# First windowed attention and two expert mixtures: K masked in blocks of 32 rows, row sums from a column of ones, the w3 half scaled on ScalarE, bias, mask and sum on GpSimd

## The reference

```python
# windowed attention: 16 heads of 8, windows of 64, each looks at itself and the window before
q, k, v = x @ Wq.T + bq, x @ Wk.T + bk, x @ Wv.T + bv
scores = einsum('bchqd,bckhd->bchqk', qc, kc) / sqrt(8)      # 64 queries against 128 keys
attn = softmax(where(valid, scores, -1e9))                   # valid: the first window of a sequence has none before it
out = einsum('bchqk,bckhd->bcqhd', attn, vc) @ Wo.T + bo
# mixture: 8 experts, the two best are used, weight s_e of the token for expert e
h  = silu((x * s_e) @ w1[e].T + b1[e])
x2 = h @ w2[e].T + b2[e]
x3 = (x * s_e) @ w3[e].T + b3[e]
y  = sum over e of x2 * x3 * mask_e
z  = (silu(x @ sw1.T) * (x @ sw2.T)) @ sw3.T                 # shared expert
out = y + z
```

## Time and profile before

| | us |
|---|---|
| median of three executions | 4510.75 |
| lowest, highest | 4509.15, 4514.94 |
| the profiled execution, whole | 4523.47 |
| its span in the profile | 4522.2 |
| windowed attention, 28.2 to 280.4 | 252.2 |
| first mixture with its norm, after its loads | 202.5 |
| second mixture with its loads | 216.0 |

### The profile page before, as it was taken

One profiled execution on the slowest core, in us unless ns is written; L12 is line 12 of the kernel. 1 busy time (PEld: TensorE's weight loads), 2 busy tenths in 40 slices (PEclk: granted clock), 3 DMA queues, 4 the chain that ended last, 5 costly groups with the idle time before them and its releaser, 6 DMA issues. The chain is left out here.

```text
span 4522.2 us, 158903 instructions
## 1 busy us (share of the span) xinstructions
PE 3865.6 (85%) x66864; PEld 2684.5 (59%) x66864; DVE 3250.0 (72%) x6705; ACT 2515.7 (56%) x4761; POOL 2493.9 (55%) x2057
## 2 busy tenths in 40 slices
PE   6858767279999999999999732899999999999996
PEld 3435544146766666666666521666666666766764
DVE  6749659577777777777778436777777777777773
ACT  2323323046767667667676401666676666767664
POOL 2211111077767677677767302766766767767662
PEclk8769979689999999999999855999999999999998
DMA  0010010033233333333322201333323333233222
GB/s 14 1 32 1 3 32 2 4 87 91 65 92 82 78 88 80 80 78 89 81 70 68 59 8 34 80 79 80 90 65 93 79 81 91 65 92 82 63 70 53
DMA packets 307779, 280.49 MB, mean 62 GB/s; under 512 B 158840, under 2 KB 205696, under 8 KB 307072
## 3 DMA queue, kind: packets, MB, share of 16 engines
q1 hardware_dynamic: 307072, 270.33, 23.5%
HBM read 55.22 MB, written 1.05 MB: 12 GB/s over the span
## 5 line engine op out<-in xcount | busy, mean ns | idle before, releaser
L1375 ACT ACTIVATE l_sq<-PS 128x512 f32<-128x512 f32 x384 | 225.9, 595 | 200.6 <-PE PS L1228 160.9
L1375 ACT ACTIVATE m_sq<-PS 128x512 f32<-128x512 f32 x384 | 225.9, 595 | 196.1 <-PE PS L1228 158.3
L1640 POOL TENSOR_TENSOR l_Pm<-l_Pm,l_rs 128x1024 f32<-128x1024 f32 x96 | 182.7, 1903 | 238.9 <-DVE l_rs L1512 238.9
L1640 POOL TENSOR_TENSOR m_Pm<-m_Pm,m_rs 128x1024 f32<-128x1024 f32 x96 | 182.7, 1904 | 236.7 <-DVE m_rs L1512 236.7
L124 POOL TENSOR_TENSOR rstd<-rstd,minus_half 128x4 f32<-128x4 f32 x40 | 41.7, 1044 | 398.1 <-DVE rstd L120 398.1
L1530 DVE TENSOR_TENSOR XN<-PS,XN 128x128 f32<-128x128 f32 x192 | 56.1, 292 | 273.0 <-PE PS L1280 273.0
L1499 DVE TENSOR_TENSOR l_QR<-PS,l_rot 128x512 f32<-128x512 f32 x192 | 131.7, 686 | 165.5 <-ACT l_sq L1375 165.5
L1499 DVE TENSOR_TENSOR m_QR<-PS,m_rot 128x512 f32<-128x512 f32 x192 | 131.8, 686 | 164.3 <-ACT m_sq L1375 164.3
L1635 POOL TENSOR_TENSOR l_QR<-l_QR,l_UQ 128x1024 f32<-128x1024 f32 x96 | 227.8, 2372 | 25.0 <-DVE l_UQ L1502 25.0
L1635 POOL TENSOR_TENSOR m_QR<-m_QR,m_UQ 128x1024 f32<-128x1024 f32 x96 | 227.7, 2372 | 24.6 <-DVE m_UQ L1502 24.6
L1635 POOL TENSOR_TENSOR l_KR<-l_KR,l_UK 128x1024 f32<-128x1024 f32 x96 | 226.8, 2362 | 0.6 <-DVE l_UK L1502 0.6
(11 more groups left out here) (387 smaller groups left out, 11817.4 us busy)
## 6 DMA issues: line engine op xcount, KB each, us to landing
l_V<-l_Vt SPq DMA_DIRECT2D x576, 128.0 KB
m_V<-m_Vt SPq DMA_DIRECT2D x576, 128.0 KB
l_V<-l_Vt SPq DMA_DIRECT2D x384, 64.0 KB
m_V<-m_Vt SPq DMA_DIRECT2D x384, 64.0 KB
l_wqkv<-l_wqkv_dram SPq DMA_DIRECT2D x72, 128.0 KB, 2.4
m_wqkv<-l_wqkv_dram SPq DMA_DIRECT2D x72, 128.0 KB, 2.4
l_rot<-l_rot_dram SPq DMA_DIRECT2D x24, 256.0 KB, 3.6
m_rot<-l_rot_dram SPq DMA_DIRECT2D x24, 256.0 KB, 3.7
```

The costliest lines, as they stand in the source:

```text
L1375: ac.activation(sq[:, c, b * 512:(b + 1) * 512], PS[:, 2 * c + b, :], ACT.Square).then_inc(sq_out)
L1640: gp.tensor_tensor(pm, pm, over(rs[:, :], 2, [P, 16, 2 * LW]), ALU.mult).then_inc(pn_out)
```

## The change

In the attention the mask has four columns in place of 16 and repeats every 32 rows. kTm then holds four copies, made by GpSimd alone, and head 4g+j is row block g (32 rows) of copy j. `scores` is one call for two banks: four matmuls of 32 rows by 64 columns by 512. v gets a ninth column of ones for each head, set once at the start, so that the value matmul yields the row's sum in its ninth column; `sums` is gone. Softmax works on halves of eight heads. The stages of a tile are spread over more turns of the loop: values run two tiles behind the scores, the transpose of the output three, the output matmul and the addition to X four; v's projection goes to bank 2, values to bank 1, the output's transpose to bank 0 and the output to bank 3. At the start of the program one fence and one wait are gone, and the attention's weights are issued behind x directly.

In the mixture w1 products fill banks 0 and 1 and w3 products banks 2 and 3. VectorE takes out the w1 half only. ScalarE takes out the w3 half, with the scale; GpSimd adds b3, multiplies by the mask, and later adds up the eight experts in three steps and adds the result to X. The shared expert's second matmul moves behind the next tile's transposes. The four gate groups get banks of their own and are taken out after the norm loop, and the choice of experts moves behind VectorE's part of the first tile.

```diff
-                headmask = sl("headmask", P, A_H)
+                headmask = sl("headmask", P, 4)
                 qT = sl("qT", P, 2, P)
                 kT = sl("kT", P, W_K)
-                kTm = sl("kTm", P, 2, A_H, W_K)
-                vc = sl("vc", P, 3, 2, D)
+                kTm = sl("kTm", P, 2, 4, W_K)
+                vc = sl("vc", P, VR, 2, A_H, A_DH + 1)
                 S = sl("S", P, 2, A_H, P)
-                pT = sl("pT", P, A_H, P)
-                mx, sm, rs = sl("mx", P, A_H), sl("sm", P, A_H), sl("rs", P, A_H)
+                pT = sl("pT", P, 2, A_H, P)
+                mx, rs = sl("mx", P, A_H), sl("rs", P, A_H)
...
+                G.step(gp.memset(vc[:, :, :, :, :], 1.0))
+                G.wait()
+                for dst, src in ((wq[:, :], t["a_wqT"]), (wk[:, :], t["a_wkT"]), (wv[:, :], t["a_wvT"]), (wo[:, :], t["a_woT"]),
+                                 (headmask[:, :], t["a_headmask"]), (bq[:, :], column("a_bq")), (bk[:, :], column("a_bk")),
+                                 (bv[:, :], row("a_bv", D)), (bo[:, :], row("a_bo", D))):
+                    sp.dma_start(dst, src).then_inc(loaded, 16)
+                sp.wait_ge(loaded, 16 * 11)
...
+                            for g in (2 * k, 2 * k + 1):
+                                rows = slice(32 * g, 32 * g + 32)
+                                m = te.matmul(PS[A_WIN * c:A_WIN * (c + 1), 4 + g, :], qT[rows, par, A_WIN * c:A_WIN * (c + 1)],
+                                              kTm[rows, par, :, A_WIN * c:A_WIN * c + P], start=True, stop=True)
...
+                        if n == 0:
+                            te.wait_ge(vc_out, min(i + 3, NT))
+                        if i >= 3 and n == 1:
+                            te.wait_ge(add_out, i - 2)
...
+                    for i in range(NT + 4):
+                        turned, valued, out = 1 <= i <= NT, 2 <= i < NT + 2, 3 <= i < NT + 3
...
+                    def exponent(i, k):
+                        sh = S[:, i % 2, 8 * k:8 * k + 8, :]
+                        ac.wait_ge(sub_out, 2 * i + k + 1)
+                        ac.activation(sh, sh, ACT.Exp, scale=float(A_DH) ** -0.5).then_inc(exp_out)
+
+                    def turned(i, n):
+                        ac.wait_ge(p_turn, 4 * i + n + 1)
+                        if i >= 2:
+                            ac.wait_ge(pv_mm, i - 1)
+                        ac.copy(pT[:, i % 2, 4 * n:4 * n + 4, :].rearrange("p a b -> p (a b)"), PS[:, 2 + n % 2, :]).then_inc(pT_out)
...
+                        for c in range(2):
+                            m = ve.tensor_tensor(vc[:, i % VR, c, :, 0:A_DH], PS[:, 2, c * P:(c + 1) * P].rearrange("p (h d) -> p h d", h=A_H),
+                                                 bv[:, :].rearrange("p (h d) -> p h d", h=A_H), ALU.add)
+                        m.then_inc(vc_out)
...
+                        V.step(ve.reciprocal(rs[:, :], got[:, :, A_DH]))
...
+                        if 3 <= i < NT + 3:
+                            divide(i - 3)
+                        if i < NT:
+                            softmax(i, 0)
+                        if i >= 4:
+                            residual(i - 4)
+                        if i < NT:
+                            softmax(i, 1)
+                        if i + 2 < NT:
+                            values_copy(i + 2)
...
-                        gp.tensor_tensor(kTm[:, par, 10:, :], over(kT[:, :], 1, [P, A_H - 10, W_K]),
-                                         over(headmask[:, 10:], 2, [P, A_H - 10, W_K]), ALU.mult).then_inc(km2_out)
-                        if i == 0:
+                            gp.wait_ge(sc_mm, 2 * (i - 1))
+                        gp.tensor_tensor(kTm[:, par, :, :], over(kT[:, :], 1, [P, 4, W_K]),
+                                         over(headmask[:, :], 2, [P, 4, W_K]), ALU.mult).then_inc(km_out)
+                        if i == 1:
...
                             turn(i - 1)
+                            shared_down(i - 1)
                         if i < NT:
                             up(i)
                         if i:
                             down(i - 1)
                         if i < NT:
-                            shared(i)
+                            shared_turn(i)
...
+                            if i >= 2:
+                                ac.wait_ge(y3_out, i - 1)
+                            if i == 0:
+                                ac.wait_ge(mask_out, 1)
+                            for n in range(2):
+                                for e in range(4 * n, 4 * n + 4):
+                                    m = ac.activation(x3[:, i % 2, e, :], PS[:, 2 + n, (e % 4) * D:(e % 4 + 1) * D], ACT.Copy, scale=sc[:, i, e:e + 1])
+                                m.then_inc(x3_out)
                             ac.wait_ge(sg_turn, i + 1)
+                            if i >= 1:
+                                ac.wait_ge(z_mm, i)
...
+                        for n in range(2):
+                            ve.wait_ge(up_mm, 5 * i + n + 1)
+                            for e in range(4 * n, 4 * n + 4):
+                                m = ve.scalar_tensor_tensor(hin[:, i % 2, e, :], PS[:, n, (e % 4) * D:(e % 4 + 1) * D], sc[:, i, e:e + 1], b1[:, e, :],
+                                                            ALU.mult, ALU.add)
+                            m.then_inc(hin_out)
...
-                        ve.tensor_tensor(y8[:, :, :], y8[:, :, :], x3[:, i % 2, :, :], ALU.mult).then_inc(x3_used)
-                        ve.wait_ge(x3_used, i + 1)
-                        V.step(ve.tensor_reduce(y1[:, :], y8[:, :, :].rearrange("p e d -> p d e"), AX, ALU.add))
-                        V.wait()
-                        ve.wait_ge(zadd_out, i + 1)
-                        V.step(ve.tensor_tensor(X[:, i, :], X[:, i, :], y1[:, :], ALU.add))
+                        ve.tensor_tensor(y, y, x3[:, i % 2, :, :], ALU.mult).then_inc(y3_out)
...
+                    for g in range(NG):
                         ve.wait_ge(gate_mm, g + 1)
-                        ve.tensor_copy(sc[:, 4 * g:4 * g + 4, :], PS[:, 1 + g % 2, 0:4 * E_N].rearrange("p (j e) -> p j e", j=4)).then_inc(gate_out)
-                    choose()
+                        ve.tensor_copy(sc[:, 4 * g:4 * g + 4, :], PS[:, 1 + g, 0:4 * E_N].rearrange("p (j e) -> p j e", j=4)).then_inc(gate_out)
+                    ve.wait_ge(gate_out, NG)
+                    scores()
+                    for i in range(NT + 1):
+                        if i:
+                            ve.wait_ge(z_mm, i)
+                            ve.tensor_tensor(X[:, i - 1, :], PS[:, 4, I_SH:I_SH + D], X[:, i - 1, :], ALU.add).then_inc(zadd_out)
+                        if i < NT:
+                            up(i)
+                            gated(i)
+                        if i == 0:
+                            choose()
+                        if i:
+                            down(i - 1)
...
+                            x = x3[:, i % 2, :, :]
+                            gp.wait_ge(x3_out, 2 * i + 2)
+                            G.step(gp.tensor_tensor(x, x, b3[:, :, :], ALU.add))
+                            G.wait()
+                            gp.tensor_tensor(x, x, over(mask[:, i, :], 2, [P, E_N, D]), ALU.mult).then_inc(x3m_out)
                         if i:
-                            down(i - 1)
-                        if i < NT:
-                            ve.wait_ge(z_mm, i + 1)
-                            ve.tensor_tensor(X[:, i, :], PS[:, 4, I_SH:I_SH + D], X[:, i, :], ALU.add).then_inc(zadd_out)
-
-                def pool():
-                    for g in range(NG):
-                        norm_root(g)
-                    for i in range(NT):
-                        gp.wait_ge(x3_out, 4 * i + 4)
-                        gp.tensor_tensor(x3[:, i % 2, :, :], x3[:, i % 2, :, :], over(mask[:, i, :], 2, [P, E_N, D]), ALU.mult).then_inc(x3m_out)
+                            y = y8[:, (i - 1) % 2, :, :]
+                            gp.wait_ge(y3_out, i)
+                            for n in (4, 2, 1):
+                                G.step(gp.tensor_tensor(y[:, 0:n, :], y[:, 0:n, :], y[:, n:2 * n, :], ALU.add))
+                                G.wait()
+                            gp.wait_ge(zadd_out, i)
+                            gp.tensor_tensor(X[:, i - 1, :], X[:, i - 1, :], y[:, 0, :], ALU.add).then_inc(tree_out)
...
-    c["a_headmask"] = (np.arange(P)[:, None] // A_DH == np.arange(A_H)[None, :]).astype(f)
+    c["a_headmask"] = (np.arange(P)[:, None] % 32 // A_DH == np.arange(4)[None, :]).astype(f)
```

More of the change, by code:

```diff
@@ L208, in project, with scores @@
                         te.matmul(PS[:, 0, P:P + W_K], wk[:, :], xw(i, 0, W_K), start=True, stop=True).then_inc(qk_mm)
[L209 to L215 removed]
+                    def scores(i, k):
                         par = i % 2
```

306 lines of the change are left out of this document (151 added, 155 removed).

## The result

| | before | after |
|---|---|---|
| median, us | 4512.84 (4509.15 to 4515.95, 4 executions) | 4435.85 (4432.96 to 4439.44, 4 executions) |
| ratio, 95% interval | | 0.983 (0.982 to 0.985) |
| span of the profiled execution | 4522.2 | 4438.1 |
| attention ends (the mixture's gate weights are loaded) | 280.4 | 253.6 |
| first mixture, loads included | 216.6 | 190.1 |

The account below looks back on a forecast made before the run. It took a ring through all engines to set the attention's tile and VectorE to bound the mixture. Attention and start 96.8 plus mixtures 42.6 make 139.4 off 4523.5, 4384; medians lying 12.7 lower, 4371 us; range 4340 to 4412.

Parts of the forecast that it names:

- So a full turn is 8.6 + 1.2: Attention: 8.6 us of TensorE work plus a 1.2 us stall awaiting the addition to X, rounded to 10.0.
- four filling turns: Attention's first turns, two paced by VectorE's 6 us and by masking the sequence's first window: 22.4 us in all.
- Rival B: Attention: TensorE's clock stays at 0.80, a turn takes 11.9 us, 25 us more, total 4396; chance 0.20.
- Rival F: Attention and mixture: many small pieces keep TensorE at 1.2 GHz; slower, 4620 at share 0.8; chance 0.03.
- Scores in row blocks: Attention: a scores call of eight 512-column matmul instructions, its four pieces side by side, takes 1.1 us.
- rival D: Attention scores: the 32-row pieces run only in pairs, 18 us more, total 4389; chance 0.10.
- GpSimd's mask: Attention: GpSimd makes the whole mask in 2.7 or 1.4 us, beside other work, costed at nothing.
- VectorE's pieces of 1024: Attention softmax: maximum and subtraction in four instructions of 1024 columns, 1.22 us each, 4.9 together.
- The start: Program start: first weight load from 8.59 to about 3.9, first arithmetic from 16.31 to 12.0, 4.3 us less.
- The mixture's tile: Mixture: 8.8 us in place of 10.12, paced by GpSimd's 7.6 plus 1.2 of mutual waiting with VectorE.
- rival C: Mixture: GpSimd and VectorE do not wait for each other, TensorE paces at 8.2 us, total 4354; chance 0.12.
- The mixture's sum: Per mixture: 6.6 + 14 x (10.12 - 8.8) - 3.8 = 21.3 us less; two make 42.6.

Follow-up runs that it names:

- experiment 1: Changed kernel with the output matmul ahead of the first scores and the addition to X ahead of the first softmax half: 4358.99 us, ratio 0.965.
- experiment 6: Changed kernel with three unread 256-column matmuls on TensorE ahead of its wait for the addition to X: 4380.92 us, ratio 0.969.
- experiment 9: Changed kernel with one unread 256-column matmul ahead of the wait for the addition to X: median 4417.98 us, profiled execution 4352.14.
- Experiment 7: Changed kernel, stall kept, with each score matmul contracting all 128 rows instead of 32: 4402.00 us, ratio 0.974.
- experiment 10: experiment 1 with VectorE doing each mixture's last-tile b3, mask, expert sum and addition to X: median 4339.35 us; profiled execution 4441.55.
- experiment 5: Changed attention and program start, with the mixture of the kernel before: 4497.39 us, ratio 0.996.
- experiment 8: Changed kernel with GpSimd's addition of b3 in the mixture left out: 4426.15 us, ratio 0.980.
- experiment 2: Changed kernel, stall kept, with value matmuls moving 32 columns per head in place of 9: 4420.28 us, ratio 0.980.

## Why the prediction was wrong, point by point

- **The failed step** is "So a full turn is 8.6 + 1.2", in the part on the attention, which the sum takes as 10.0 us: the turns took 15.1, at a granted clock of 0.50. Work and stall were nearly right: 8.2 us at full clock (experiment 1) and a stall of 1.21. What failed is that the stall was added as time and not also weighed as what takes the clock away. Experiments 1 and 6 show it: without the stall, or with the stall filled, the clock stays at 1.00 in the stage's middle.
- **What the step would have given.** The execution of experiment 9 that kept its clock and most of its waiting puts the attention's end at 186.7 us. The prediction put it at 280.4 - 96.8 = 183.6, so the sum for a kept clock was right within 3 us, in part by luck. Its full turns take 9.6 us in place of 10.0, but the four filling turns take 31.3 (first maximum of the first and of the fifth tile at 29.49 and 60.77) in place of 22.4, some of it at the low clock.
- **Rival B** (the clock stays at the attention's present 0.80) took a mean over the stage for a property of it. In the earlier trace rows the clock falls to 0.53 and is back at 1.00 within a tile, when the 128-row scores follow. Experiment 7 has 128-row scores behind the same stall and reads 0.93. The change removed what brought the clock back. I had put the fall down to four microseconds of short work alone, but TensorE also stood idle in them: 1.16 us before the values (in the earlier trace rows, one tile on), and then

```profile
102.70 0.33 PE L252 MATMUL PS<-ident,a_o 128*128 128x128 f32 x1 [0.92 <-DVE a_o L356]
103.39 0.80 PE L254 MATMUL PS<-a_wo,a_oT 128*128 128x128 f32 x2 [0.35 <-ACT a_oT L301]
```

  The output's transpose takes 0.33 us, as it does at full clock in the changed kernel, and the output matmul behind it 0.80, as at the low one. So the trace of before already had a clock that fell behind an idle microsecond.
- **Rival F** named the mechanism, small pieces at 1.2 GHz, with chance 0.03, because it was tied to the mixture too and priced at 4620. In the attention alone, 13 turns of 15.1 in place of 10.0 (the prediction's count) cost 66 of the 70 us missed there. Against it I had set the 1.00 "of most of the attention tile", which was 128-row work. The Trainium skill, TensorE: Matmul & The Clock Gate, section "Part 1: The HAM clock gate (the "warmup" mystery)", lets an array that stays busy have its full clock back; here 192 us without a gap did not bring it back (experiment 10; 191.3 of 192 us busy in experiment 5), so busy in the profile's sense is not what the gate goes by.
- **Scores in row blocks:** the forecast of 1.1 was right and rival D fell: 1.09 us a call, the four pieces run side by side, and 1.98 at half the clock.
- **GpSimd's mask:** 1.467 us, near the lower price (1.4); VectorE no longer works on K beside it.
- **VectorE's pieces of 1024:** 1.225 us, as worked out from the earlier trace rows.
- **The start:** the first weight load at 4.00, the first arithmetic at 12.34, 4.0 us earlier; 4.3 forecast.
- **The mixture's tile** was mis-sized: 8.8 forecast, 8.03 measured, against

```profile
L623 DVE TENSOR_TENSOR f_sg<-f_sg,PS x16: 420/422/423, 294.8 to 425.0; 128x256 f32<-128x256 f32 x16
```

  whose second is at 312.04: 112.96 us for 14 tiles, 8.07 each. GpSimd does not set it (experiment 8), TensorE does. The waiting for each other is real, but smaller:

```profile
L635 DVE TENSOR_TENSOR f_y<-f_y,f_x x16: 1226/1576/3386, 314.2 to 435.7; 128x1024 f32<-128x1024 f32 x16
L666 POOL TENSOR_TENSOR f_x<-f_x,f_b x16: 2341/2358/3336, 303.8 to 431.3; 128x1024 f32<-128x1024 f32 x16
```

```profile
L673 POOL TENSOR_TENSOR f_y<-f_y 128x256 f32<-128x256 f32 x14 | 16.3, 1166 | 1.1
L673 POOL TENSOR_TENSOR f_y<-f_y 128x128 f32<-128x128 f32 x13 | 8.6, 660 | 1.0
L676 POOL TENSOR_TENSOR X<-X,f_y 128x128 f32<-128x128 f32 x13 | 7.7, 592 | 1.0
```

  These three rows are from 300 to 430 us. What the mean lies above the shortest or the forecast price is 0.44 for 256 columns (0.73 in the earlier trace rows), 0.20 and 0.14 for 128 (0.46, 0.453), and 0.13 for the b3 addition (mean 2.468 in that stretch): 0.9 us a tile in place of 1.2. With the 7.2 of the forecast's prices that is 8.1, so GpSimd and TensorE lie within 0.1 us of each other; the 0.4 us that the forecast added for GpSimd's waits on itself do not show. This was rival C's number, for half of its reason: the two engines do wait for each other, but TensorE sets the pace.
- **The mixture's sum:** the last gate copy comes 33.7 us after the loads against 39.6, 5.9 less (6.6 forecast). (The forecast's own terms, 1.1 + 0.6 + 1.9, add up to 3.6 a group and not 3.7.) From it to the second gated product 24.7 us against 24.0. The loop 14 x (10.12 - 8.07) = 28.7 less (18.5). From the last gated product to the next loads 18.7 against 11.2, 7.5 more (3.8). Together 5.9 - 0.7 + 28.7 - 7.5 = 26.4; 26.5 measured.

## What to carry to other kernels

Before work on TensorE is made thinner (fewer rows, fewer columns), look in the trace of before for short stalls in that stage and at what brings the clock back behind each: if it is the work that the change thins, one stall can cost the clock for the whole stage. A forecast must then price a new stall at its length and, apart from that, at all the work behind it at half speed. The cheap cures here were order (the producer of the awaited result goes first) and, where a wait must stay, matmuls that nobody reads; a profile of one execution is not enough where the clock has two outcomes.

## What the runs showed of the hardware

- A stage of 32-row scores and 9-column values ran in two ways. At 2.4 GHz a turn takes 8.0 to 8.2 us, at 1.2 GHz 15.1, and TensorE is almost without gaps in both. In no profile did full turns leave either while TensorE was busy: 112 us at 1.00 in experiment 1, 192 at 0.50 in experiment 10.
- An idle stretch of 1.21 us lost the clock in both profiles in which thin work without a fill met it at full clock (the changed kernel, experiment 8). Its length alone does not decide: behind one matmul of filling, stretches of 0.69 and one of 1.41 us left the clock at 1.00 (experiment 9, the profiled execution; three others took 53 to 90 us longer), and with wider values or scores stretches of 1.2 us lost it at some times and not at others (experiments 2 and 7).
- More array work can save time: scores over 128 rows instead of 32 cost 0.85 us a call and made the kernel 34 us faster; 1.3 us of unread matmuls per turn made it 55 us faster.
- What exactly the gate measures was not settled. 32 columns in place of 9 brought the clock back after 51 us at first and later after 7 to 14, 128 rows in place of 32 within the turn each time; narrower steps between were not tried, nor an idle stretch of the same length with nothing else changed around it.
